# A graph and mixture-of-experts stack: where degrees, own rows, mask, roots and the last head's squares are computed

## The reference, cut to what matters

```python
# layer 0, graph: a normalised neighbour sum
deg  = segment_sum(ones, col)                 # col: edges plus one loop per node
dinv = rsqrt(deg)
h    = x @ W
out  = segment_sum(h[row] * (dinv[row] * dinv[col])[:, None], col) + b

# layer 0, feed-forward: 12 heads of attention, then the experts
xn     = rmsnorm(x, norm1_w)
qkv    = xn.reshape(b, s, 12, 64).transpose(0, 2, 1, 3)
scores = qkv @ qkv^T / 8;  attn = softmax(scores);  ao = attn @ qkv
out    = x + attn_out
xf     = rmsnorm(out, norm3_w)                # feeds the router, a shared expert and 8 experts
```

## Time and profile before

| | us |
|---|---|
| median of 3 runs | 1620.09 |
| lowest, highest | 1619.05, 1623.38 |
| the profiled execution, whole | 1621.49 |
| its span in the trace | 1619.9 |
| TensorE busy | 1474.3 (91%) |
| VectorE busy | 1263.2 (78%) |
| ScalarE busy | 873.3 (54%) |
| POOL busy | 332.4 (21%) |
| mean granted TensorE clock | 0.959 |

### The profile page before, as it was taken

The page is one execution under the profiler, slowest core; times in us unless marked ns, Lnnn a source line. Parts: engine busy times, 40 slices in busy tenths (PEclk is TensorE's granted clock), DMA queues, the critical chain, the costliest instruction groups (busy, mean ns, idle before and its releaser), DMA issues.

```text
span 1619.9 us, 36985 instructions
## 1 busy us (share of the span) xinstructions
PE 1474.3 (91%) x14673; PEld 1271.2 (78%) x14673; DVE 1263.2 (78%) x2191; ACT 873.3 (54%) x1235; POOL 332.4 (21%) x254
## 2 busy tenths in 40 slices
PE   7988968885999999999999889866999999999996
PEld 5666756664767899999998644445999999999994
DVE  8998477774565688888888679867988888888785
ACT  1113257776344567776775135554666665666651
POOL 0000416562040000000004047753600000000050
PEclk9999979997999999999999779977999999999999
DMA  7640000002475788888886011126888888888883
GB/s 203 157 121 1 11 0 1 1 1 98 138 231 174 253 276 300 302 297 296 305 286 197 1 32 32 33 88 214 280 311 285 301 285 296 302 290 295 294 267 96
DMA packets 55557, 297.61 MB, mean 184 GB/s; under 512 B 14064, under 2 KB 14320, under 8 KB 32434
## 3 DMA queue, kind: packets, MB, share of 16 engines
q1 hardware_dynamic: 41761, 263.23, 47.9%
q0 software_dynamic: 13712, 33.26, 7.6%
HBM read 264.07 MB, written 32.34 MB: 183 GB/s over the span
## 4 chain that ended last, share of the span: by engine, by line
PE 69%; DVE 19%; ACT 4%; issue 3%; POOL 2%; DMA 2%; SPq 0%; POOLq 0%; DVEq 0%; ACTq 0%
PE ps L744 14%; PE ps L723 9%; PE ps L725 9%; PE ps L727 9%; PE ps L2274 5%; PE ps L2257 5%; DVE wl L1396 3%; DVE wl L1397 3%; PE ps L2386 2%; POOL wl L996 2%; DMA ext<-in_units 2%; PE ps L2186 2%; DVE wl L600 2%; PE ps L756 1%; PE ps L2172 1%
## 5 line engine op out<-in xcount | busy, mean ns | idle before, releaser
L723 PE MATMUL ps<-big,wh 128*128 128x176 f16 x2160 | 496.3, 240 | 9.0 <-DVE wl L600 5.2
L727 PE MATMUL ps<-big,wl 128*128 128x176 f16 x2160 | 496.4, 238 | 0.0
L725 PE MATMUL ps<-big,wh 128*128 128x176 f16 x2160 | 496.3, 238 | 0.0
L744 PE MATMUL ps<-big,wh 128*128 128x176 f16 x2160 | 262.7, 238 | 3.8 <-DVE big L634 3.8
L744 PE MATMUL ps<-big,wl 128*128 128x176 f16 x1080 | 248.9, 239 | 0.0
L600 DVE SCALAR_TENSOR_TENSOR wl<-ext,wh 128x2304 f16<-128x2304 f32 x90 | 229.7, 2552 | 1.5 <-issue 0.9
L600 DVE SCALAR_TENSOR_TENSOR wl<-raw,wh 128x2304 f16<-128x2304 f32 x90 | 229.5, 2550 | 0.0
L519 ACT ACTIVATE wh<-raw 128x2304 f16<-128x2304 f32 x90 | 190.4, 2117 | 57.5 <-PE ps L744 53.7
L723 PEld LDWEIGHTS ps<-big,wh 128*128 128x128 f16 x2160 | 208.7, 97 | 12.8 <-issue 4.3
L519 ACT ACTIVATE wh<-ext 128x2304 f16<-128x2304 f32 x90 | 190.5, 2117 | 51.2 <-PE ps L744 35.6
L725 PEld LDWEIGHTS ps<-big,wh 128*128 128x128 f16 x2160 | 211.2, 98 | 0.2
(11 more groups left out here) (363 smaller groups left out, 2814.5 us busy)
## 6 DMA issues: line engine op xcount, KB each, us to landing
raw<-in_units SPq DMA_DIRECT2D x54, 1152.0 KB
ext<-in_units SPq DMA_DIRECT2D x54, 1152.0 KB
raw<-in_units SPq DMA_DIRECT2D x36, 1153.0 KB, 5.9
ext<-in_units SPq DMA_DIRECT2D x36, 1153.0 KB, 6.4
raw<-in_units_s SPq DMA_DIRECT2D x16, 769.0 KB, 4.6
ext<-in_units_s SPq DMA_DIRECT2D x16, 769.0 KB, 4.5
x_slots<-raw SPq DMA_DIRECT2D x1, 8976.0 KB
big<-x_slots POOLq DMA_DIRECT2D x17, 528.0 KB, 8.6
```

What stands on the lines that cost most here:

```text
L723: nc.tensor.matmul(o, wh[:, u % RING, w_], x_, start=c == 0 and m == 0, stop=False, skip_group_check=True)
L725: nc.tensor.matmul(o, wh[:, u % RING, w_], xTl[:, c, 0:ph.n], start=False, stop=False, skip_group_check=True)
L727: ins = nc.tensor.matmul(o, wl[:, u % RING, w_], x_, start=False, stop=c == KC - 1, skip_group_check=True)
L744: ins = nc.tensor.matmul(o, l_[:, u % RING, w_], r_, start=first and k == 0 and c % 2 == 0, stop=last and k == 2, skip_group_check=True)
```

## The change

1. **Degrees from a spare one-hot column.** The source's one-hot row is written over 626 places instead of 628, so columns 626 and 627 keep a 1.0 from a memset. The last block of counts thereby gets a row (partition 126) of in-degrees. The unpacking runs over 127 partitions instead of 125. TensorE transposes the last block of CT five times in fp32 and VectorE reads the degrees; the 50 one-column matmuls go. The root is asked ahead of the pass that makes CTh, and VectorE does the bias additions partly ahead of the root's chain, partly behind it, and CTl behind both.
2. **Own rows added by VectorE.** The identity matmuls of the aggregation go; after each `node_low` VectorE adds the own row to xres (one operation over 768 columns per tile). TensorE's third and fourth product tiles now wait for that addition.
3. **Mask from fp16 counts.** The transposes read CTh in fp16 and alternate between two banks.
4. **Roots ahead of ScalarE's passes.** The roots of tile t+1 are asked before the inverses of tile t are finished, and ScalarE takes them before the three passes of tile t.
5. **The last tile's heads apart.** Of tile 4, head 0 is split first, heads 1 to 11 after the first `side_out`, before the first maximum (VectorE) and the first exponential (ScalarE).
6. **Layer 0's last head squared apart.** The squares are taken in four parts: heads 0-3 during head 6, heads 4-7 during head 10, heads 8-10 after the last exponentials, head 11 behind the fence. VectorE adds head 11's sum to z itself, and multiplies by the norm weights before the fence (704 columns, then 64). `sum_out(H - 2)` stands before the last `weight_high`.

```diff
-                nc.vector.tensor_scalar(hot[0:P, s, 0:TP], iota16[:, :], edges_f[:, 0, c:c + 1], None, ALU.is_equal)
+                nc.vector.tensor_scalar(hot[0:P, s, 0:ROWS], iota16[:, 0:ROWS], edges_f[:, 0, c:c + 1], None, ALU.is_equal)
...
# ScalarE
-            act.wait_ge(s_unp, 3 * len(GROUPS))
+            root()
             nc.scalar.activation(CTh, CT, ACT.Copy).then_inc(s_nh, 1)
-            root()
...
+            both_roots(0)
+            for t in range(NT):
+                if t + 1 < NT:
+                    both_roots(t + 1)
                 count["sq"] += 1
                 act.wait_ge(s_var, count["sq"])
...
+                if t + 1 < NT:
+                    heads_high(t, 0, H)
+                    row_out(t)
+            heads_high(NT - 1, 0, 1)
             side_out(0)
+            heads_high(NT - 1, 1, H)
+            row_out(NT - 1)
...
+                if h in (6, 10):
+                    if t == 0:
+                        act.wait_ge(s_madd, h - 2)
+                    squares((h - 6) // 4, t)
+            sum_out(H - 2)
             weight_high(H * NT - 1)
-            sum_out(H - 2)
+            act.wait_ge(s_madd, H - 1)
+            for t in range(NT):
+                squares(2, t)
             sum_out(H - 1)
             fence(act, F_MHA)
...
-            squares()
+            act.wait_ge(s_madd, H)
+            for t in range(NT):
+                squares(3, t)
             root()
# VectorE
             def node_low(t):
...
+                nc.vector.scalar_tensor_tensor(out=xres[:, t, :], in0=node_sum(t), scalar=rs[:, 2, t:t + 1],
+                                               in1=xres[:, t, :], op0=ALU.mult, op1=ALU.add).then_inc(s_aggv, 1)
...
-            fin(H - 1)
+            dve.wait_ge(s_vec[0], 32)
+            dve.wait_ge(s_madd, H - 1)
+            row_weighted(0, PARTS[3])
+            dve.wait_ge(s_mback, H)
+            for t in range(NT):
+                ins = nc.vector.scalar_tensor_tensor(
+                    out=z[:, t, PARTS[3]:D], in0=bank(7)[0:P, 128 + t * HD:128 + (t + 1) * HD],
+                    scalar=cols[:, 4 + (H - 1) % 2, t:t + 1], in1=z[:, t, PARTS[3]:D], op0=ALU.mult, op1=ALU.add)
+            ins.then_inc(s_madd, 1)
+            dve.wait_ge(s_madd, H)
+            step(row_weighted(PARTS[3], D))
             fence(dve, F_MHA)
# TensorE
-            for i in range(NT):
-                for part in (CTh, CTl):
-                    for k in range(NT):
-                        ins = nc.tensor.matmul(bank(6)[0:P, i:i + 1], part[:, k, i * P:(i + 1) * P], iota16[0:P, 1:2],
+            node_products(1, 0, BANK)
+            pe.wait_ge(s_unp, 3 * len(GROUPS))
+            for i in range(NT):
+                ins = nc.tensor.transpose(degree_rows()[:, i, 0:PD], CTD[:, NT - 1, i * P:(i + 1) * P],
+                                          ident[0:PD, 0:PD])
+            ins.then_inc(s_deg, 1)
+            node_products(1, BANK, D)
+            for t in range(2, NT):
+                if t >= 3:
+                    pe.wait_ge(s_aggv, t - 2)
                 node_products(t, 0, BANK)
+                if t == 2:
+                    pe.wait_ge(s_var, 2)
+                    pe.wait_ge(s_nh, NH_CT + 1)
+                counts_turned(2 * t - 4)
                 node_products(t, BANK, D)
+                if t < 4:
+                    counts_turned(2 * t - 3)
...
-                        nc.tensor.matmul(o, ident16[0:P, 0:P], r_[:, i, n0:n1], start=False, stop=False)
```

More of the change, by code:

```diff
@@ L27 @@
 TP, TH, TQ = 628, 314, 157
+PD, ROWS = P + 2, 626
 FIELD = 4096.0
@@ L159, in bass_gnn_moe_stack @@
         xsl = region(big, KC * T // 2, KC * T // 2).bitcast(F16).rearrange("p (c n) -> p c n", c=KC)
-        junk = [big[0:P, (t if t < 4 else 6) * D:((t if t < 4 else 6) + 1) * D] for t in range(NT)]
+        junk = [big[0:P, (t * D if t < 4 else 6700):(t * D if t < 4 else 6700) + D] for t in range(NT)]
         yT = region(big, 0, KC * B).rearrange("p (c n) -> p c n", c=KC)
@@ L1019, in root, with squares @@
                 nc.scalar.activation(rs[:, 1, :], rs[:, 0, :], ACT.Sqrt).then_inc(s_sq, 1)
-            def squares():
-                count["sq"] += 1
-                act.wait_ge(s_var, count["sq"])
-                for t in range(NT):
-                    ins = nc.scalar.activation(junk[t], z[:, t, :], ACT.Square, accum_out=rs[:, 0, t:t + 1])
-                ins.then_inc(s_sq, 1)
+            def squares(g, t):
+                own = slice(PARTS[g], PARTS[g + 1])
+                nc.scalar.activation(junk[t][:, own], z[:, t, own], ACT.Square,
+                                     accum_out=st[:, t, g, 0:1]).then_inc(s_part, 1)
             def rows_high(half):
@@ L1076, in _, with both_roots @@
             act.wait_ge(s_logs, 3)
-            for t in range(NT):
+            def both_roots(t):
                 count["sq"] += 1
@@ L1488, in node_low @@
                                                in1=hth[:, t, :], op0=ALU.mult, op1=ALU.subtract).then_inc(s_nl, 1)
+                nc.vector.scalar_tensor_tensor(out=xres[:, t, :], in0=node_sum(t), scalar=rs[:, 2, t:t + 1],
+                                               in1=xres[:, t, :], op0=ALU.mult, op1=ALU.add).then_inc(s_aggv, 1)
             def masked_counts(i):
                 dve.wait_ge(s_cT, i + 1)
-                nc.vector.tensor_scalar(mask[:, i, :].rearrange("p (k n) -> p k n", k=NT), tiles5(bank(6, 2), P), 0.0,
+                nc.vector.tensor_scalar(mask[:, i, :].rearrange("p (k n) -> p k n", k=NT), counts_back(i), 0.0,
                                         NEG, ALU.is_equal, ALU.mult).then_inc(s_cdv, 1)
-            for t in range(NT):
-                node_low(t)
-                masked_counts(t)
+            node_low(0)
+            node_low(1)
+            masked_counts(0)
+            masked_counts(1)
+            node_low(2)
+            masked_counts(2)
+            masked_counts(3)
+            node_low(3)
+            masked_counts(4)
+            node_low(4)
             def summed(t):
@@ L2089, in _ @@
             pe.wait_ge(s_unp, 3 * len(GROUPS) - 2)
-            for t in range(2):
+            for n0, n1 in ((0, BANK), (BANK, D)):
+                node_products(0, n0, n1)
+            node_products(1, 0, BANK)
[5 more added lines that the diff above has]
+            node_products(1, BANK, D)
+            for t in range(2, NT):
+                if t >= 3:
+                    pe.wait_ge(s_aggv, t - 2)
                 node_products(t, 0, BANK)
+                if t == 2:
+                    pe.wait_ge(s_var, 2)
+                    pe.wait_ge(s_nh, NH_CT + 1)
+                counts_turned(2 * t - 4)
                 node_products(t, BANK, D)
+                if t < 4:
+                    counts_turned(2 * t - 3)
             pe.wait_ge(s_nl, NL_CT + 1)
-            for i in range(NT):
-                for part in (CTh, CTl):
-                    for k in range(NT):
-                        ins = nc.tensor.matmul(bank(6)[0:P, i:i + 1], part[:, k, i * P:(i + 1) * P], iota16[0:P, 1:2],
-                                               start=part is CTh and k == 0, stop=part is CTl and k == NT - 1)
-            ins.then_inc(s_deg, 1)
-            pe.wait_ge(s_var, 2)
-            counts_turned(0)
-            for t in range(2, NT):
-                if t == 3:
-                    pe.wait_ge(s_nl, NL_H + 1)
-                if t == 4:
-                    pe.wait_ge(s_nl, NL_H + 2)
-                node_products(t, 0, BANK)
-                if t == 4:
-                    counts_turned(3)
-                node_products(t, BANK, D)
-                counts_turned(t - 1 if t < 4 else 4)
             pe.wait_ge(s_nl, NL_H + NT)
             for i in range(NT):
-                if i >= 2:
-                    pe.wait_ge(s_aggv, i - 1)
+                pe.wait_ge(s_aggv, NT + i - 1)
                 for n0, n1 in ((0, BANK), (BANK, D)):
```

109 lines of the change are left out of this document (64 added, 45 removed).

## The result

The changed kernel takes 1608.64 us (median of 11 runs, 1603.04 to 1615.40) against 1621.35 (11 runs of the kernel before beside it): a ratio of 0.9917, 95% interval 0.9898 to 0.9936. On two further chips it was 0.9940 (0.9917 to 0.9962) and 0.9912 (0.9883 to 0.9940). The forecast was 1608. Its profiled execution took 1606.14 us, its span 1604.6 against 1619.9.

What follows compares the result with a forecast made beforehand. Idle waits in node products, aggregation and attention's end were taken to bound 134 to 394 us. 5.5 - 1.9 + 1.3 + 3.2 - 0.1 - 0.3 + 4.2 = 11.9 us off 1621.49, then 1.4 to the median: 1608; range 1603.5 to 1613.

Steps and rivals of the forecast that it cites:

- Part 1: Edge matrix: the one-hot row over 626 instead of 628 columns, 165 times, keeps its rate; gain 0.
- The rival of the lost rate: Edge matrix: 165 one-hot rows over 626 columns at +0.16 us each, 25 us on the path, 1633; chance 0.05.
- Part 2: Degrees and own rows up to the aggregation: start 5.5 us sooner, less 1.9 for a clock fall behind TensorE's new stop.
- Part 3: Aggregation: shorter TensorE groups bring the second sum 1.3 us sooner; four waits of 0.8 for a root go, 3.2.
- Part 4: Last inverse to first exponential: head 0 comes sooner but the table load is no longer hidden; -0.1, bounds -1 and +1.5.
- Part 5: Squares in attention heads 6 and 10, on a partly idle ScalarE: -0.3, bounds 0 and -4.1.
- the rival of squares on attention's path: Attention: nearly all ten squares land on the path, 1612; chance 0.17 shared with turn or own rows falling short.
- Part 6: End of attention to the scaled rows: earlier last sums and shorter squares behind the fence gain 4.2 us, bounds 3 and 5.6.
- It doesn't do what it says: Before aggregation: CTl and bias additions give back the degrees' gain; own rows may hold tile 4; 1610 to 1612; shared 0.17.

Runs made afterwards that it cites:

- the experiment without the stop: Low counts and two bias additions moved later on VectorE and GpSimd released later, against the changed kernel: 1604.88 us.

## Why the prediction was right

The sum was 11.9 us up to the scaled rows. The first trace has 13.69 (393.46 against 379.77), the other two 11.55 and 11.29. By its parts, in the first trace:

- **Part 1**, 0: 376 against 373 ns. The rival of the lost rate falls, and with it the only way to 1633.
- **Part 2**, 5.5 - 1.9: the start at 184.77 instead of 189.10, 4.33; forecast 185.5. The stop is 2.92 (forecast: 3) and the fall costs 1.70 (forecast: 1.9; 27.78 against 26.08). That the clock would fall was held likelier than not; it fell in six of seven runs. Tile 3's products were put at 168.8 and start at 168.20; from there the prediction had 14.8 us to the aggregation, and it is 16.57, 14.87 without the fall. The trace of before has a fall of its own, at 163: its tile 2 takes 7.99 us (the row below) where tile 3 takes 6.02. Of the 5.89 us by which tile 3 starts sooner, some 2.0 are that fall; whether it comes in every run of the kernel before, one trace can't show.

```profile
165.72 7.99 PE L2073 MATMUL ps<-raw,big 128*125 128x512 f16 x36
```

- **Part 3**, 1.3 + 3.2: 4.49 (35.54 against 31.05), and 2.8 where the clock falls in the first group, which the prediction did not price. Undoing the roots takes 3.15 of it and leaves the 1.3. The 3.2 were put down to two conditions, the root taken early and TensorE's shorter groups, and both were needed: with only the roots early the turn is 5.5 us.
- **Part 4**, -0.1: -0.21, and the undoing shows -0.15 and another -0.2 in attention.
- **Part 5**, -0.3: 0.0; the rival of squares on attention's path falls by forty squares that cost nothing.
- **Part 6**, 4.2: 5.07 with the clock held in the last sums, 3.4 to 3.8 with it fallen, as it was before. The prediction assumed it fallen, so like for like it is 0.4 to 0.8 too high. The squares are 2.90 of it (the prediction: 4.26 - 1.3 = 2.96); but from the last division to the squares it takes 1.94 us (373.84 to 375.78), where the prediction had 1.5.

The mechanisms held: the stop, the fall behind it, the turn without its wait, the squares. Taken with the falls that the prediction assumed (one at 168, one in the last sums, none at the aggregation), the marks add up to 4.3 + 4.5 - 0.2 + 3.7 = 12.3 us against 11.9; no single run of the changed kernel had that pattern.

That 1608.64 lies so near 1608 is luck in good part. The falls of the clock make some 3 us between the first trace and the other two (1.69 at the aggregation, 1.3 to 1.4 in the last sums), and the rest of the program scatters by 11. The prediction carried the gain at 394 us to the end unchanged, which no single pair of runs could confirm. "It doesn't do what it says" was half right in mechanism: the bias additions and CTl did take back most of the degrees' 7.3 us, and the experiment without the stop shows that 4.8 us could be had by another order. Its other half did not come: the own rows did not hold tile 4.

## What to carry to other kernels

Work that is moved to an idle engine pays less where it is put ahead of what another engine waits for: in the order in which they lengthened TensorE's stop the own rows earned an estimated 1.9 us at a held clock and 0.3 or less in the traces, and 2.8 us in the order without the stop. Two changes in one loop have to be tried together: each alone gave about half of what it gave behind the other. A root asked one tile earlier is a change of a few lines that took a wait of 0.8 us out of every turn. When an order on VectorE is changed, look also at when GpSimd is released: its pass should not fall on operations that read two operands in SBUF (8.09 us for one of 0.95 here). And where marks in the trace repeat to hundredths of a us while times scatter by 10, judge parts by marks.

## What the runs showed of the hardware

- **VectorE and GpSimd exclude each other while VectorE reads two operands in SBUF.** A bias addition with both operands in SBUF, started 0.75 us behind GpSimd's pass, took 8.09 us instead of 0.95. GpSimd's next pass, started 0.36 us behind VectorE's low counts, took 9.70 us instead of 6.80; the low counts ended 3.05 us into it. With GpSimd released later both were back at their lengths. An operation with one of its two operands in PSUM took its 1.00 us in the midst of a pass. The Trainium skill ("SBUF — State Buffer", "Who interferes with whom" and "Summary: rules for kernel authors") says that a VectorE instruction with two SBUF inputs contends with a GpSimd instruction that reads SBUF, and that the second to issue is blocked until the first ends. The rows agree on who is blocked, but not on until when, and that stays open: the blocked addition ended at 173.81 and the next one took its 0.95 us from 173.73, while GpSimd's pass is recorded until 175.78.
- **Short stops let TensorE's clock fall in some runs and not in others.** Behind a stop of 2.9 us it fell in six of seven runs, behind one of 2.1 us (before the aggregation) in eight of thirteen, of 2.0 us in none of one; each of these falls to 1.2 GHz cost 1.7 us. In all five runs without the stop ahead of tile 3 the 18 matmuls there took 4.05 us. Ahead of the last weighted sums TensorE stands for 1.5 us (1.0 in one run, where the clock held) behind ten matmuls of 64 columns, and the clock fell in nine of thirteen runs, for 1.3 to 1.7 us. What decides it in a run was not found.
